# More rows fetched one by one, two gather buffers and undivided VectorE copies in a recommendation kernel

## The chip, the cores and the metric

The kernel runs on one core of one Trainium2 chip. The metric is the device time of one execution in microseconds (us), as the median of several runs.

## The reference

For each of 2048 samples, 26 embedding rows of 64 numbers are looked up in 26 tables of 12,500 rows. A 27th vector comes from the price by a dense layer. All products of two of the 27 vectors go, with the output of a small network over the dense vector, through two last layers.

```python
emb = emb_tables[jnp.arange(NUM_FIELDS)[:, None], x_cat]      # 26 x 2048 x 64
emb = jnp.transpose(emb, (1, 0, 2))
dense_embed = price[:, None] @ Wp + bp
feats = jnp.concatenate([emb, dense_embed[:, None, :]], axis=1)
gram = jnp.einsum('bid,bjd->bij', feats, feats)
interactions = gram[:, _IU, _JU]                              # 351 pairs
h = jax.nn.relu(dense_embed @ W1 + b1)
dense_out = jax.nn.relu(h @ W2 + b2)
concat = jnp.concatenate([interactions, dense_out], axis=1)
t = jax.nn.relu(concat @ Wt1 + bt1)
out = (t @ Wt2 + bt2)[:, 0]
```

## The kernel before, in words

The 2048 samples are 16 tiles of 128. Sample s of a tile sits on partition s, and for each tile and each of the 26 fields one column of 64 numbers per partition has to be fetched. Most columns are fetched by GpSimd with one indirect DMA each (`gather`, L274), which takes its 128 row numbers from `row_idx`. Fifteen of the 416 columns, all of them field 24 or field 25, are instead fetched row by row: SyncE issues 128 single DMAs of 256 bytes for field 25 of the nine tiles in `SP_TILES`, and ScalarE does so for field 24 of the six tiles in `ACT_TILES` (`fetch_rows`, L175 loads up to 32 addresses into registers, L178 issues the DMAs). The addresses lie on one partition in `by_row_at`, and VectorE computes them at the start from a second copy of the indices (`row_addresses`).

ScalarE can't issue its rows in one go, since it has other work: `fetch_some(n)` issues the next n rows of its list at fixed places of its program. There are 24 rows ahead of tile 0, and in each tile 32 after the first chunk, 12 after the second, 12 after the first round of copies and 8 after the second, until the list of 768 rows is empty.

A tile is worked on in this order. Its columns come in two chunks (fields 0 to 13, fields 14 to 25). For each chunk TensorE transposes pairs of fields into `ps_trans` (L553). VectorE copies the even fields and ScalarE the odd ones into `feats` (`evacuate_chunk`, L212); both have to be done before the next chunk is transposed. ScalarE also writes the dense vector into `feats` (`dense_slots`, L313). Then come two rounds of Gram products: 32 matmuls into the four banks of `ps_gram` (L600), and 16 copies of 32x112 numbers out of it into `gram` (`evacuate_gram`, L203), eight by VectorE (quads 0, 1) and eight by ScalarE (quads 2, 3). The next round waits for all 16. `gathered` has one buffer, so GpSimd may fetch a chunk of tile t only once TensorE has transposed that chunk of tile t-1.

Tiles form batches (0-3, 4-7, 8-11, 12-13, 14-15). At the first tile of the next batch, between its first and second chunk, TensorE does `top_layer` for the batch before (L627, L632; two halves of 7 matmuls with 2 passes each), ScalarE applies the relu to the first half (L368), VectorE to the second (L501), and the scores follow (L653, L378). Tile 14 is done in four finer rounds (L621, L200). Tile 15 is laid out in four units of 32 samples, each with its own gathers, transposes (L574), round and copies (L198), so that little is left after the last gather. Each engine has a fixed program order, and engines wait for each other only through semaphores.

Of the kernel before, what the change touches and what calls it, by code (L numbers as in the profile page):

```python
# [8 lines left out]
P = 128  # L9
# [34 lines left out]
ROW_TILES = SP_TILES + ACT_TILES  # L44
PAIRS = sorted(set(ROW_TILES))
REGS = 32
FIRST_ROWS, AFTER_FIRST_CHUNK, AFTER_CHUNKS, AFTER_ROUND = 24, 32, 12, (12, 8)
# [12 lines left out]
def rec_kernel(nc, price, x_cat, x_rows, table, consts, w1, w2, wt1_pairs, wt1_dense, out):  # L60
# [3 lines left out]
    with ExitStack() as ctx:  # L64
# [47 lines left out]
        by_row_loaded = sem("by_row_loaded")  # L112
        sp_rows_made = sem("sp_rows_made")
        act_rows_made = sem("act_rows_made")
        sp_fetched = [sem(f"sp_fetched{n}") for n in range(len(SP_TILES))]
        act_fetched = [sem(f"act_fetched{n}") for n in range(len(ACT_TILES))]
        base_made = sem("base_made")
        idx_step = sem("idx_step")
# [38 lines left out]
        def by_gpsimd(t, f):  # L157
            return not (f == SP_FIELD and t in SP_TILES or f == ACT_FIELD and t in ACT_TILES)

# [12 lines left out]
        def fetch_rows(eng, name, t, f, at, p0, n, done):  # L172

            row_of = [eng.alloc_register(f"{name}_{t}_{p0 + k}") for k in range(n)]
            eng.load(row_of, by_row_at[:, at + p0:at + p0 + n])  # L175
            for k in range(n):
                row = eng.snap(row_of[k], min_val=0, max_val=(FIELDS * VOCAB - 1) * ROW_BYTES, donate=True)
                eng.dma_start(field_at(t, f, 1)[p0 + k:p0 + k + 1, :].bitcast(u8), table_bytes[:, bass.ds(row, ROW_BYTES)])\  # L178
                    .then_inc(done, 16)
# [35 lines left out]
        def evacuate_unit(copy, n, kk):  # L215
# [29 lines left out]
        def _(sp):  # L245
            sp.dma_start(raw_idx[:, 0:FIELDS], x_cat[:, 0:FIELDS]).then_inc(first_idx_loaded, 16)
            sp.dma_start(raw_idx[:, FIELDS:], x_cat[:, FIELDS:]).then_inc(idx_loaded, 16)
            sp.dma_start(by_row_raw[:, :], x_rows).then_inc(by_row_loaded, 16)
# [3 lines left out]
            for n, t in enumerate(SP_TILES):  # L252
                sp.wait_ge(sp_rows_made, 1 if n == 0 else 2)
                for p0 in range(0, P, REGS):
                    fetch_rows(sp, "sp_row", t, SP_FIELD, n * P, p0, REGS, sp_fetched[n])
# [8 lines left out]
        def _(pool):  # L264
# [13 lines left out]
            for t in range(LAST):  # L278
# [4 lines left out]
                for c, (f0, f1) in enumerate(CHUNKS):  # L283
# [3 lines left out]
                    if t > 0:  # L287
                        pool.wait_ge(chunk_transposed[c], t)
# [4 lines left out]
            pool.wait_ge(rows_made, 2 + 3 * UNITS)  # L293
            pool.wait_ge(chunk_transposed[0], LAST)
            for n in range(UNITS):
                if n == 2:
                    pool.wait_ge(chunk_transposed[1], LAST)
                for col in UNIT_COLS[n]:
                    gather(LAST, col, unit_gathered[n])

        @block.scalar
        def _(act):
# [13 lines left out]
            issued = [0]  # L316
# [448 lines left out]
```

## Time and profile before

| | |
|---|---|
| median of 3 runs | 525.09 us (524.4 to 525.5) |
| profiled execution | 524.21 us, of which the span of the trace is 522.3 us |
| GpSimd busy | 381.2 us (73%) |
| TensorE busy | 247.1 us (47%) |
| ScalarE busy | 167.7 us (32%) |
| VectorE busy | 153.5 us (29%) |

Issuing a DMA is not counted as busy time. A gather counts with what GpSimd does for it (0.95 us), but a row DMA that SyncE or ScalarE issues shows only as a row of the queue (SPq, ACTq). So the busy time of ScalarE tells less than half of what fills it. The span is 1.9 us shorter than the time of the same execution.

### The profile page before, as it was taken

How to read it: one execution, taken by the hardware profiler on the slowest of the kernel's cores; microseconds unless marked ns; L12 is line 12 of the kernel's file. 1: busy time of each engine (PE TensorE's matmuls, PEld its weight loads, DVE VectorE, ACT ScalarE, POOL GpSimd, SP SyncE). 2: the span in 40 equal slices, each digit the busy share in tenths (PEclk: the TensorE clock that was granted, in tenths of full speed). 3: DMA queues.
4: the chain of work that ended last, by engine and by line, in shares of the span. 5: the costliest groups of instructions: out<-in, count | busy, mean ns of one | idle time of the engine just before them, and what ended most of it. 6: DMA issues, size and time to landing. Idle time of an engine off the chain costs nothing.

```text
span 522.3 us, 8323 instructions
## 1 busy us (share of the span) xinstructions
PE 247.1 (47%) x1481; PEld 181.6 (35%) x1481; DVE 153.5 (29%) x399; ACT 167.7 (32%) x413; POOL 381.2 (73%) x408
## 2 busy tenths in 40 slices
PE   0004436154548661432516954151432894469487
PEld 0003324132333350422415434050422543356375
DVE  6203303123140141241304024042241315332753
ACT  0032513335142141242404225042242425342743
POOL 6777777777777777777777776777777777777770
PEclk9999755666578855566656976555566896668789
DMA  6333332333323333333333332333333333332110
GB/s 191 26 28 29 28 29 28 28 29 28 28 28 29 29 28 28 30 27 30 28 30 26 29 28 24 29 30 27 28 28 30 27 29 27 29 28 27 28 26 4
DMA packets 17754, 16.52 MB, mean 32 GB/s; under 512 B 10772, under 2 KB 11028, under 8 KB 17574
## 3 DMA queue, kind: packets, MB, share of 16 engines
q0 software_dynamic: 12832, 13.17, 30.6%
q1 hardware_dynamic: 2886, 2.49, 1.6%
q10 hardware_dynamic: 1984, 0.34, 0.4%
q14 instruction: 40, 0.33, 0.3%
q8 instruction: 12, 0.20, 0.2%
HBM read 15.95 MB, written 0.01 MB: 31 GB/s over the span
## 4 chain that ended last, share of the span: by engine, by line
ACTq 31%; POOL 19%; PE 19%; issue 16%; ACT 13%; DMA 2%; DVE 1%; POOLq 0%
ACTq L178 26%; POOL gathered L274 18%; PE ps_gram L600 10%; ACT gram L203 9%; PE ps_mlp L632 5%; ACTq L175 4%; ACT feats L212 2%; ACT feats L313 1%; DMA gathered<-in_table,row_idx 1%; PE ps_trans L553 1%; PE ps_trans L632 1%; PE ps_mlp L627 0%; ACT dense_out L363 0%; PE ps_mlp L584 0%; DMA raw_idx<-in_x_cat 0%
## 5 line engine op out<-in xcount | busy, mean ns | idle before, releaser
L274 POOL DMA_INDIRECT gathered<-in_table,row_idx x394 | 373.8, 949 | 124.9 <-issue 118.9
L600 PE MATMUL ps_gram<-feats 64*128 64x128 f32 x896 | 101.9, 414 | 137.3 <-issue 79.3
L600 PEld LDWEIGHTS ps_gram<-feats 64*128 64x128 f32 x896 | 95.4, 317 | 150.9 <-issue 144.3
L203 DVE COPY gram<-ps_gram 32x112 f32<-32x112 f32 x224 | 80.4, 359 | 197.5 <-PE ps_gram L600 194.8
L203 ACT COPY gram<-ps_gram 32x112 f32<-32x112 f32 x224 | 80.9, 361 | 116.3 <-PE ps_gram L600 84.2
L553 PE MATMUL ps_trans<-ident,gathered 128*128 128x128 f32 x184 | 39.9, 378 | 119.2 <-DMA gathered<-in_table,row_idx 71.9
L212 ACT COPY feats<-ps_trans 64x448 f32<-64x448 f32 (+1 forms) x60 | 34.1, 569 | 164.5 <-issue 121.6
L553 PEld LDWEIGHTS ps_trans<-ident,gathered 128*128 128x128 f32 x184 | 30.6, 197 | 131.3 <-issue 131.2
L212 DVE COPY feats<-ps_trans 64x448 f32<-64x448 f32 (+1 forms) x60 | 36.3, 604 | 94.8 <-PE ps_trans L553 94.0
L632 PE MATMUL ps_mlp<-gram,wt1p_sb 128*128 128x512 f32 (+2 forms) x140 | 54.7, 552 | 1.7 <-ACT gram L203 1.7
L632 PEld LDWEIGHTS ps_mlp<-gram,wt1p_sb 128*128 128x128 f32 x140 | 28.8, 222 | 27.6 <-issue 22.5
L501 DVE TENSOR_SCALAR top<-ps_mlp,consts_sb 128x512 f32<-128x512 f32 (+1 forms) x4 | 2.7, 684 | 52.0 <-PE ps_mlp L632 52.0
L313 ACT ACTIVATE feats<-price_bc,consts_sb 64x64 f32<-64x64 f32 x30 | 14.7, 491 | 0.8
L621 PE MATMUL ps_gram<-feats 64*128 64x128 f32 x128 | 9.9, 301 | 10.1 <-ACT feats L222 4.4
L621 PEld LDWEIGHTS ps_gram<-feats 64*128 64x128 f32 x128 | 8.6, 204 | 11.9 <-DVE feats L222 7.8
L627 PE MATMUL ps_mlp<-dense_out,wt1d_sb 64*128 64x512 f32 (+2 forms) x20 | 10.0, 586 | 3.5 <-ACT dense_out L363 3.5
L198 DVE COPY gram<-ps_gram 32x56 f32<-32x56 f32 x32 | 8.2, 256 | 10.2 <-PE ps_gram L621 9.8
L198 ACT COPY gram<-ps_gram 32x56 f32<-32x56 f32 x32 | 8.3, 259 | 6.3 <-PE ps_gram L621 6.0
L212 ACT ACT_TABLE_LOAD x1 | 1.3, 1283 | 26.9 <-issue 26.9
L200 DVE COPY gram<-ps_gram 32x56 f32<-32x56 f32 x32 | 8.3, 258 | 1.7 <-PE ps_gram L621 1.3
L200 ACT COPY gram<-ps_gram 32x56 f32<-32x56 f32 x32 | 8.3, 260 | 1.3 <-PE ps_gram L621 0.9
L368 ACT ACTIVATE top<-ps_mlp,consts_sb 128x512 f32<-128x512 f32 (+1 forms) x4 | 2.5, 634 | 18.0 <-PE ps_mlp L632 18.0
(54 smaller groups left out, 100.3 us busy)
## 6 DMA issues: line engine op xcount, KB each, us to landing
pairs_of<-in_table SPq DMA_DIRECT2D x1152, 0.2 KB
pairs_of<-in_table ACTq DMA_DIRECT2D x768, 0.2 KB
gathered<-in_table,row_idx POOLq DMA_INDIRECT x394, 3.4
price_bc<-in_price SPq DMA_DIRECT2D x1, 1024.0 KB, 5.7
wt1p_sb<-in_wt_pairs SPq DMA_DIRECT2D x1, 896.0 KB, 7.8
raw_idx<-in_x_cat SPq DMA_DIRECT2D x1, 195.0 KB, 2.7
pairs_of<-in_table,row_idx POOLq DMA_INDIRECT x7
w_sb<-in_w ACTq DMA_DIRECT2D x2, 32.0 KB, 3.1
```

The costliest lines, as they stand in the source:

```text
L175: eng.load(row_of, by_row_at[:, at + p0:at + p0 + n])
L178: eng.dma_start(field_at(t, f, 1)[p0 + k:p0 + k + 1, :].bitcast(u8), table_bytes[:, bass.ds(row, ROW_BYTES)])\
L198: last = copy(gram_unit[to, w, k, r, :, :, :, s], fine_from[part, r % 2, :, :, s, 0:SLABS, c])
L200: last = copy(gram_to[to, w, k, :, FINE_RG * r:FINE_RG * (r + 1), :, s], fine_from[part, r % 2, :, :, s, 0:SLABS, c])
L203: last = copy(gram_to[to, w, k, :, RG * r:RG * (r + 1), :, s], gram_from[part, :, :, s, 0:SLABS, c])
L212: last = copy(feats[D * h:D * (h + 1), :, 1 + f0 + q:f1 + q:2], src[D * q:D * (q + 1), h, :, :])
L274: pool.indirect_dma_start(out=field_at(t, f, 1), out_offset=None, in_=rows, in_offset=bass.IndirectOffsetOnAxis(ap=row_idx[:, at:at + 1], ...
L313: return nc.scalar.activation(dst, price_bc[part, first:first + n], ACT.Identity, bias=const(BP, part), scale=const(WP, part))
L553: last = nc.tensor.transpose(ps_trans[:, to + k * P:to + (k + 1) * P], field_at(t, f, 2), ident[:, :])
L600: last = nc.tensor.matmul(ps_gram[:, out_at:out_at + P], group, group, start=True, stop=True)
L621: last = nc.tensor.matmul(ps_gram[:, to:to + P], group, group, start=True, stop=True)
L632: last = nc.tensor.matmul(to, wt1p_sb[:, j * TM1 + m * P:j * TM1 + (m + 1) * P], gram[:, at + part.start:at + part.stop], start=False, sto ...
```

## The change

1. Seventeen columns instead of fifteen are fetched row by row. SyncE has 1208 rows: field 25 of eight tiles, 104 rows of tile 14 and 80 rows of tile 15. ScalarE has 968 rows: field 24 of tiles 2, 4, 6, 7, 9, 11, 13, and the remaining 24 and 48 rows of field 25 of tiles 14 and 15. GpSimd issues 399 gathers, before 401.
2. ScalarE issues 36 rows ahead of tile 0 (now before it waits for the small inputs), then 32 after the first chunk and 40 after the second chunk of each tile; none between the rounds of copies.
3. In tiles 0 to 11 VectorE makes all 16 copies of each Gram round. From tile 12 on the two engines share them as before.
4. `gathered` has two buffers: a chunk of tile t waits for the transposes of tile t-2.
5. The addresses on one partition come from 17 matmuls, which turn columns of `row_idx` into rows, and five scalings by VectorE; the second copy of the indices is gone. The clamp of the indices takes three instructions instead of four, and for the long part it works in PSUM. The base numbers of tile 15 are laid out once.
6. The order of fields in the units of tile 15 changes, and with it the address pattern of the copies in `evacuate_unit`.

```diff
-BUFFERS = 1
+BUFFERS = 2
-SP_TILES = (2, 4, 5, 7, 8, 10, 11, 13, 14)
-ACT_TILES = (2, 4, 6, 8, 10, 12)
+SPLIT_ROWS = {LAST - 1: 104, LAST: 80}
+SP_TILES = (2, 4, 5, 7, 8, 10, 11, 13)
+ACT_TILES = (2, 4, 6, 7, 9, 11, 13)
+SP_ROWS = [(t, SP_FIELD, 0, P) for t in SP_TILES] + [(t, SP_FIELD, 0, n) for t, n in SPLIT_ROWS.items()]
+ACT_ROWS = [(t, ACT_FIELD, 0, P) for t in ACT_TILES] + [(t, SP_FIELD, n, P - n) for t, n in SPLIT_ROWS.items()]
-FIRST_ROWS, AFTER_FIRST_CHUNK, AFTER_CHUNKS, AFTER_ROUND = 24, 32, 12, (12, 8)
+VECTOR_ALONE = 12
+FIRST_ROWS, AFTER_FIRST_CHUNK, AFTER_CHUNKS = 36, 32, 40
...
-                    if t > 0:
-                        pool.wait_ge(chunk_transposed[c], t)
+                    if t >= BUFFERS:
+                        pool.wait_ge(chunk_transposed[c], t - BUFFERS + 1)
...
             def fetch_some(n):
-                if issued[0] == 0:
-                    act.wait_ge(act_rows_made, 1)
-                while n > 0 and issued[0] < len(ACT_TILES) * P:
-                    k, p0 = divmod(issued[0], P)
-                    now = min(n, P - p0, REGS)
-                    fetch_rows(act, "act_row", ACT_TILES[k], ACT_FIELD, (len(SP_TILES) + k) * P, p0, now, act_fetched[k])
-                    issued[0] += now
-                    n -= now
+                for t, f, first, rows in ACT_ROWS:
+                    while n > 0 and issued[t, f, first, rows] < rows:
+                        done = issued[t, f, first, rows]
+                        now = min(n, rows - done, REGS)
+                        act.wait_ge(addresses_made, address_group(t, f) + 1)
+                        fetch_rows(act, "act_row", t, f, first + done, now)
+                        issued[t, f, first, rows] += now
+                        n -= now
...
                 fetch_some(AFTER_CHUNKS)
-                for r in range(ROUNDS if t < LAST - 1 else FINE_ROUNDS):
-                    gram_round(r, t)
-                    if r < ROUNDS:
-                        fetch_some(AFTER_ROUND[r])
+                if t >= VECTOR_ALONE:
+                    for r in range(ROUNDS if t < LAST - 1 else FINE_ROUNDS):
+                        gram_round(r, t)
...
             def gram_round(r, t):
                 dve.wait_ge(gram_done, rounds_before(t) + r + 1)
-                evacuate_gram(nc.vector.tensor_copy, t, r, (0, 1)).then_inc(gram_evac_dve, 1)
+                evacuate_gram(nc.vector.tensor_copy, t, r, range(GROUP) if t < VECTOR_ALONE else (0, 1))\
+                    .then_inc(gram_evac_dve, 1)
...
+            pe.wait_ge(by_row_picked, 1)
+            for k, (t, f) in enumerate(BY_ROW):
+                col = 2 * t + f - ACT_FIELD
+                summed = nc.tensor.matmul(address_sums(k * P, (k + 1) * P), by_row_idx[:, col:col + 1], ident[:, :],
+                                          start=True, stop=True)
+                if (k + 1) % AT_ONCE == 0 or k == len(BY_ROW) - 1:
+                    summed.then_inc(addresses_summed, 1)
+            pe.wait_ge(addresses_made, ADDRESS_GROUPS)
...
             def wait_gram_evac(n):
                 if n > 0:
                     pe.wait_ge(gram_evac_dve, n)
-                    pe.wait_ge(gram_evac_act, n)
+                if n > ROUNDS * VECTOR_ALONE:
+                    pe.wait_ge(gram_evac_act, n - ROUNDS * VECTOR_ALONE)
```

On ScalarE (ACT), before, tile 11 ends with its last eight rows and 16 copies, and tile 12, which begins with the copies of the first chunk and has the top layer, holds no row at all:

```order
L175 TENSOR_LOAD by_row_at
L178 DMA pairs_of<-in_table 1x256 x8
L203 COPY gram<-ps_gram 32x2x8x7 x16
L212 COPY feats<-ps_trans 64x64x7 x2
L313 ACTIVATE feats<-price_bc,consts_sb 64x64 x2
L368 ACTIVATE top<-ps_mlp,consts_sb 128x512
L212 COPY feats<-ps_trans 64x64x6 x2
L378 ACTIVATE scores<-ps_mlp,consts_sb 1x512
L203 COPY gram<-ps_gram 32x2x8x7 x16
```

The same place on ScalarE after the change: tile 12 from the copies of its first chunk to the copies of its Gram rounds.

```order
L223 COPY feats<-ps_trans 64x64x7 x2
L320 ACTIVATE feats<-price_bc,consts_sb 64x64 x2
L375 ACTIVATE top<-ps_mlp,consts_sb 128x512
L186 TENSOR_LOAD by_row_at
L189 DMA pairs_of<-in_table 1x256 x20
L186 TENSOR_LOAD by_row_at
L189 DMA pairs_of<-in_table 1x256 x12
L223 COPY feats<-ps_trans 64x64x6 x2
L385 ACTIVATE scores<-ps_mlp,consts_sb 1x512
L186 TENSOR_LOAD by_row_at
L189 DMA pairs_of<-in_table 1x256 x32
L186 TENSOR_LOAD by_row_at
```

What moved: 68 rows and four loads now stand in tile 12, 32 rows between the relu and the copies of the second chunk, and 36 (the last four behind a load of their own, just past the end of the piece) between those and the 16 Gram copies.

On ScalarE in a middle tile, before (tile 10, from the copies of its first chunk to the end of its rows; the 12 rows after the second chunk stand as one load here):

```order
L212 COPY feats<-ps_trans 64x64x7 x2
L313 ACTIVATE feats<-price_bc,consts_sb 64x64 x2
L175 TENSOR_LOAD by_row_at
L178 DMA pairs_of<-in_table 1x256 x32
L212 COPY feats<-ps_trans 64x64x6 x2
L175 TENSOR_LOAD by_row_at
L178 DMA pairs_of<-in_table 1x256 x12
L203 COPY gram<-ps_gram 32x2x8x7 x8
L175 TENSOR_LOAD by_row_at
L178 DMA pairs_of<-in_table 1x256 x12
L203 COPY gram<-ps_gram 32x2x8x7 x8
```

And after the change, tile 11 of ScalarE, the middle tile with the most loads:

```order
L223 COPY feats<-ps_trans 64x64x7 x2
L320 ACTIVATE feats<-price_bc,consts_sb 64x64 x2
L186 TENSOR_LOAD by_row_at
L189 DMA pairs_of<-in_table 1x256 x32
L223 COPY feats<-ps_trans 64x64x6 x2
L186 TENSOR_LOAD by_row_at
L189 DMA pairs_of<-in_table 1x256 x32
L186 TENSOR_LOAD by_row_at
L189 DMA pairs_of<-in_table 1x256 x4
```

What moved: the Gram copies are gone from ScalarE, and all rows of the tile's second half stand in one run (32+8 in most tiles, 32+4+4 in this one) ahead of the next tile's first copies.

## Rows read from the trace of the kernel before

**Rows 1.** The page: granted TensorE clock in 40 slices of 13 us, tenths of full.

```profile
PEclk9999755666578855566656976555566896668789
```

**Rows 2.** Timeline of GpSimd: start, duration, what, idle time before it.

```profile
3.92 1.10 POOL L274 DMA_INDIRECT gathered<-in_table,row_idx  x1 [2.32 <-DVE row_idx L448]
...
12.61 1.56 POOL L274 DMA_INDIRECT gathered<-in_table,row_idx  x1 [0.30 <-issue]
...
493.15 0.94 POOL L274 DMA_INDIRECT gathered<-in_table,row_idx  x1 [0.30 <-issue]
```

**Rows 3.** Who waited for whom: total us, times, longest.

```profile
POOL gathered L274 <- issue: 118.9, 389, 0.5
POOL gathered L274 <- PE ps_trans L553: 3.6, 4, 1.9
```

**Rows 4.** The chain that ended last, its last gather: start, duration, what.

```profile
506.87 0.94 POOL gathered L274
```

**Rows 5.** Timeline of ScalarE: one run of 12 rows in tile 9, then tile 10.

```profile
338.03 4.97 ACTq L178 DMA_DIRECT2D pairs_of<-in_table  x12
...
354.62 1.26 ACT L212 COPY feats<-ps_trans 64x448 f32<-64x448 f32 x2 [1.65 <-issue]
355.90 1.01 ACT L313 ACTIVATE feats<-price_bc,consts_sb 64x64 f32<-64x64 f32 x2
356.95 10.56 ACTq L178 DMA_DIRECT2D pairs_of<-in_table  x32
367.55 1.03 ACT L212 COPY feats<-ps_trans 64x384 f32<-64x384 f32 x2 [10.64 <-issue]
368.69 4.25 ACTq L178 DMA_DIRECT2D pairs_of<-in_table  x12
...
384.57 1.26 ACT L212 COPY feats<-ps_trans 64x448 f32<-64x448 f32 x2 [1.65 <-issue]
```

**Rows 6.** Loads and row DMAs by source line: ns min/median/max, first and last start.

```profile
L175 ACTq TENSOR_LOAD <-by_row_at x52: 580/954/2295, 17.1 to 397.5; - x52
L178 SPq DMA_DIRECT2D pairs_of<-in_table x1152: 227/228/457, 7.6 to 465.7; - x192
```

**Rows 7.** Timeline of TensorE: a Gram round of tile 9.

```profile
346.02 3.79 PE L600 MATMUL ps_gram<-feats 64*128 64x128 f32 x32 [4.01 <-ACT gram L203]
```

**Rows 8.** Timeline of VectorE: eight copies of one Gram round.

```profile
311.85 2.83 DVE L203 COPY gram<-ps_gram 32x112 f32<-32x112 f32 x8 [9.04 <-PE ps_gram L600]
```

**Rows 9.** Timeline of ScalarE, the top layer in tile 8, and the start of tiles 5 and 12.

```profile
197.38 1.26 ACT L212 COPY feats<-ps_trans 64x448 f32<-64x448 f32 x2 [1.94 <-issue]
...
293.71 0.69 ACT L368 ACTIVATE top<-ps_mlp,consts_sb 128x512 f32<-128x512 f32 x1 [2.41 <-PE ps_mlp L632]
...
306.89 1.03 ACT L212 COPY feats<-ps_trans 64x384 f32<-64x384 f32 x2 [12.50 <-issue]
...
412.29 1.28 ACT L212 COPY feats<-ps_trans 64x448 f32<-64x448 f32 x2
```

**Rows 10.** Timeline of TensorE: tile 8's top layer, then from tile 13 to the last unit.

```profile
287.42 6.25 PE L632 MATMUL ps_mlp<-gram,wt1p_sb 128*128 128x512 f32 x14 [0.46 <-ACT gram L203]
...
437.48 1.75 PE L553 MATMUL ps_trans<-ident,gathered 128*128 128x128 f32 x7
447.08 1.30 PE L553 MATMUL ps_trans<-ident,gathered 128*128 128x128 f32 x5 [7.85 <-DMA pairs_of<-in_table,row_idx]
...
456.83 3.55 PE L600 MATMUL ps_gram<-feats 64*128 64x128 f32 x32 [3.34 <-ACT gram L203]
465.37 1.73 PE L553 MATMUL ps_trans<-ident,gathered 128*128 128x128 f32 x7 [4.99 <-DMA gathered<-in_table,row_idx]
...
487.41 0.55 PE L574 MATMUL ps_trans<-ident,gathered 128*128 128x128 f32 x3
...
495.52 0.87 PE L574 MATMUL ps_trans<-ident,gathered 128*128 128x128 f32 x3 [0.94 <-DMA gathered<-in_table,row_idx]
...
510.66 0.55 PE L574 MATMUL ps_trans<-ident,gathered 128*128 128x128 f32 x3 [0.28 <-DMA gathered<-in_table,row_idx]
```

More of the change, by code:

```diff
@@ L111, in rec_kernel @@
         idx_loaded = sem("idx_loaded")
[L112 to L116, printed above, removed]
+        by_row_picked = sem("by_row_picked")
+        addresses_summed = sem("addresses_summed")
+        addresses_made = sem("addresses_made")
+        row_fetched = {at: sem(f"row_fetched_{at[0]}_{at[1]}") for at in BY_ROW}
         base_made = sem("base_made")
+        last_base_made = sem("last_base_made")
         idx_step = sem("idx_step")
@@ L157, in by_gpsimd @@
         def by_gpsimd(t, f):
-            return not (f == SP_FIELD and t in SP_TILES or f == ACT_FIELD and t in ACT_TILES)
+            return (t, f) not in BY_ROW
         def gathers_before(c, t):
@@ L247, in _ @@
             sp.dma_start(raw_idx[:, FIELDS:], x_cat[:, FIELDS:]).then_inc(idx_loaded, 16)
-            sp.dma_start(by_row_raw[:, :], x_rows).then_inc(by_row_loaded, 16)
             sp.dma_start(price_bc[:, :], price.rearrange("(o b) -> o b", o=1).to_broadcast([P, BATCH])).then_inc(price_loaded, 16)
             sp.dma_start(wt1p_sb[:, :], wt1_pairs).then_inc(pairs_loaded, 16)
[L252 to L255, printed above, removed]
+            for t, f, first, n in SP_ROWS:
+                sp.wait_ge(addresses_made, address_group(t, f) + 1)
+                for p0 in range(first, first + n, REGS):
+                    fetch_rows(sp, "sp_row", t, f, p0, min(REGS, first + n - p0))
             for late in range(2):
@@ L559, in transpose_chunk @@
                 pe.wait_ge(chunk_gathered[c], 16 * gathers_before(c, t + 1))
-                if t in SP_TILES and f1 > SP_FIELD:
-                    pe.wait_ge(sp_fetched[SP_TILES.index(t)], 16 * P)
-                if t in ACT_TILES and f1 > ACT_FIELD:
-                    pe.wait_ge(act_fetched[ACT_TILES.index(t)], 16 * P)
+                for f in range(f0, f1):
+                    if not by_gpsimd(t, f):
+                        pe.wait_ge(row_fetched[t, f], 16 * P)
                 transpose_fields(t, f0, f1, 0).then_inc(chunk_transposed[c], 1)
@@ L569, in transpose_unit @@
                 keep_warm(n, n % 2)
-                pe.wait_ge(unit_gathered[n], 16 * len(UNIT_COLS[n]))
+                pe.wait_ge(unit_gathered[n], 16 * sum(by_gpsimd(LAST, col) for col in UNIT_COLS[n]))
+                for col in UNIT_COLS[n]:
+                    if not by_gpsimd(LAST, col):
+                        pe.wait_ge(row_fetched[LAST, col], 16 * P)
                 base = (LAST % BUFFERS) * ROW
                 for m in range(COLS // 2):
-                    at, to = base + UNIT_COLS[n][2 * m] * D, BANK * (n % 2) + m * P
-                    last = nc.tensor.transpose(ps_trans[:, to:to + P], gathered[:, at:at + 2 * D], ident[:, :])
+                    to = BANK * (n % 2) + m * P
+                    last = nc.tensor.transpose(ps_trans[:, to:to + P], field_at(LAST, UNIT_COLS[n][2 * m], 2), ident[:, :])
                 if n % 2 == 0:
@@ L737 @@
     last = cat[:, -1].reshape(FIELDS, UNITS, 2, SIDE)
-    own = last[:SHARED].reshape(COLS, UNITS, UNITS, 2, SIDE).transpose(1, 3, 4, 2, 0).reshape(P, UNITS, COLS)
+    own = last[:SHARED].reshape(UNITS, COLS, UNITS, 2, SIDE).transpose(0, 3, 4, 2, 1).reshape(P, UNITS, COLS)
     shared = last[SHARED:].reshape(2, 2, 2, 2, SIDE).transpose(2, 0, 3, 4, 1).reshape(P, 2)
```

125 lines of the change are left out of this document (65 added, 60 removed).

## The prediction

> **What bounds the kernel now.** I read the timeline of GpSimd first, since most columns come through it. Its gathers start every 1.247 us ((506.87-493.15)/11, [rows 2, 4]) from 3.92 to 506.87 us, and 400 such steps are 498.8 of these 503 us. The rest is about 2 us in the first 15 us, where single gathers take up to 1.56 us [rows 2], and waits: 389 of its idle times are the plain 0.3 us of issue, and four, 3.6 us together, wait for the transposes that free the only buffer [rows 3]. So GpSimd sets the end, and behind its last gather 15.4 us are left.
>
> The second view is the timeline of ScalarE, and it says that something else is almost as long. I call the start of a tile's first ScalarE copies A0 and that of its second A1. In tile 10, A0 is at 354.62, 32 rows are issued, A1 is at 367.55, and the next A0 at 384.57 [rows 5]: 29.95 us a tile, filled with 64 row issues and 16 copies, where GpSimd needs 30 to 31 us for 24 or 25 gathers. That a single buffer costs GpSimd only four waits shows how close the race is. Whatever lengthens the path of ScalarE and TensorE is therefore what I have to price.
>
> **Terms.** One row costs ScalarE 10.56/32 = 0.33 us; a 32-row run with its load takes 12.93 us from A0 to A1, the copies hidden in the load [rows 5]. A run of 8 costs a load (0.7, between the least and the median) and 8 x 0.33: 3.3 us; a run of 4 costs 2.0. A field border inside a run adds 0.7 (4.97 against 4.25 us for 12 rows) [rows 5, 6]. A Gram round is 3.8 us of matmuls in the middle [rows 7], a first-chunk transpose 1.75 [rows 10]. Sixteen copies by VectorE alone do not occur in the trace. Bounds: 5.7 us (twice the 2.83 of eight, [rows 8]) if they run as now, and 2.83 if one engine could do 16 in the time of 8, for which no row speaks; I take 5.8, since eight also take a little longer in other rounds.
>
> **Gathers.** Two fewer, 2.5 us; the four waits go, 2.4 us beyond issue; the first gather can start 0.2 us sooner (one dependent VectorE step less). Of the 2 us at the start I keep 0.7, bounds 0 and 2.0: the gathers stretch where VectorE works on long vectors. The last gather then starts at 3.7+0.7+398 x 1.247 = 500.7 instead of 506.87. *SBUF — State Buffer* in the Trainium skill (SBUF: two separate sides) says that VectorE and GpSimd share a port pair as an exclusive lock, taken by operations with two inputs in SBUF or in a two-port mode. The stretched gathers beside such operations agree, and by that rule the copies from PSUM, now doubled, cost the gathers nothing; mid-kernel gathers take 0.94 us [rows 2].
>
> **The middle tiles.** After A1 there are two legs up to the next A0. ScalarE: 32 rows 12.9 and 8 rows 3.3, together 16.2. TensorE and VectorE: copies 1.03, round 3.8, copies 5.8, round 3.8, transposes 1.75, some 0.3 of handing over, together 16.5. So a tile is 12.9+16.5 = 29.4 us, half a microsecond less than before: eight more rows have replaced the copies. The first four tiles are paced by gathers and the same ScalarE load, and tile 4's top layer, waiting 0.5 us longer for VectorE, starts about where it did; I put A0 of tile 5 where it was, 197.4 [rows 9].
>
> Three steps bring A0 of tile 8 to 285.6. Its top layer needs the copies of tile 7's second round, which VectorE ends 20.55 after A1 of tile 7 (copies 1.03, then round, 16 copies, round, 16 copies, and handing over), so at 269.1+20.55 = 289.7; before, eight copies sufficed. Its first half takes 6.3 us [rows 10], relu at 295.9, then 13.2 to A1 as before (293.71 to 306.89, [rows 9]) and 0.7 for a border: 309.8. A0 of tile 9 is 326.3, of 10 355.7, of 11 385.8 (border), and of 12 415.6 (A1 398.7, then runs of 32, 4 and 4: 16.9). Before it was 412.3 [rows 9]. A lag of up to 20 us behind the gathers does not stop GpSimd, for with two buffers it may be a whole tile ahead.
>
> **Tile 12** is where I expect the change to be decided. Before, the list of rows was empty by then, the last load being at 397.5 [rows 6], and from A0 at 412.29 to the transposes of tile 13 took 25 us [rows 9, 10]. Now 36+12x72 = 900 of 968 rows are out, and 68 are left, ahead of Gram copies that ScalarE shares again from this tile on. VectorE ends tile 11 at 398.7+20.55 = 419.3; relu 425.6; 32 rows with a border, A1 at 439.5. Then 36 rows, 12.9+2.0, to 454.4; only now ScalarE's copies of the first round, 3.0, and TensorE's second round, 3.9. Tile 13's transposes start at 461.3, against 437.48.
>
> **From there to the end** nothing waits for gathers any more. ScalarE's copies of the round end at 464.4, the chunk's at 465.7, the second transposes start at 465.8. From there to tile 14's first is 13.3 us (447.08 to 456.83+3.55): 479.1. Tile 14 to the first unit took 22.04, of which 0.3 waited, and gets 0.5 more since ScalarE's copies are not done ahead: 501.4. First to last unit took 23.25 with 1.2 of waiting for gathers: 523.4. The last unit to the end is 11.64 [rows 10]. That is a span of 535.1 and a time of 537.0; the profiled execution lay 0.9 under the median, so **537.9 us**.
>
> **What is free.** SyncE: 1152 rows took 458.1 us, so 12.7 us per 32 with a load [rows 6]; 1208 rows in 39 runs take 484, and starting near 12 us (indices landed by 5, some 5 us of VectorE and TensorE steps, a load) they end near 496, with the last unit not wanted before 523. If TensorE were on time (504) there would be 8 us left. Later addresses (matmuls, the memset of `feats` ahead of the scalings) cost ScalarE's first 36 rows nothing, as they end by about 25 us, when the first chunk is there. The new copy pattern of the units has the same element counts.
>
> *Trainium Kernel Development and Optimization* in the Trainium skill (Key Constraints) says that issuing DMAs from several engines only saves the sequencer's issue time. That speaks against this change: a column moved off GpSimd frees 1.25 us there and fills some 42 us (128 x 0.33) of another queue, and ScalarE's is the one that the copies stand behind.
>
> **Rivals.** (a) *The gathers stay the bound.* Last gather 500.7, last unit 3.8 later at 504.5, span 516.1, median 518.9: faster. It needs the last unit 18.9 us sooner than my path. For it speaks that GpSimd bounds the kernel today. A row cost of 0.26 us would do: near the 0.23 that the queue shows for one row DMA alone [rows 6], cycles of 27 us, the lag of each top layer gone before the next. Against it, the long runs of the trace cost 0.33 apiece and more [rows 5].
> (b) *TensorE at its upper clock.* Slices 6 to 39 mostly show 0.5 to 0.7 of full [rows 1], a mix of the two levels 1.2 and 2.4 GHz, and the 3.8 us rounds are at the lower. At 2.1 us each round, both top layers start 3.4 us sooner, and tiles 4, 12 and 13 give as much again: about 17 us less, 521. Against it, TensorE will idle longer between rounds than now.
> (c) *Slower still.* ScalarE's rows in one unbroken run could cost 0.35 instead of 0.33, or 16 copies 6.2: 1 to 1.4 us per tile more, 545 to 550.
> (d) *The delays cancel.* If the path is about 12.7 us shorter than I sum it, the last unit is ready at 510.7 and nothing changes: 525.
>
> **Numbers.** My case 0.73, with its own range 530 to 546; (a) 0.12, (b) 0.05, (c) 0.06, (d) 0.04. A measurement tells about 0.2% (1 us) from no change. Faster: (a) and (b), 0.17. Same: most of (d), 0.03. Slower: the rest, 0.80. The range reaches from 524 to 547, leaving out (a), (b) and half of (c).
>
> **What would show it.** In the changed trace, GpSimd's last gather near 500.7, without waits. A0 of tiles 5, 8, 12 near 197, 286, 416, 29.4 us apart between. In tile 12 two row runs around A1, ScalarE's Gram copies ending near 457, and the first transposes of tile 13 near 461, some 28 us after their gathers. A last unit that waits for no DMA, near 523, and a chain that ended last without GpSimd in its final 20 us. I am wrong if a run of 32 rows takes 10 us with its load, if Gram rounds in the middle take 2.1 us, or if GpSimd's last gather ends less than 5 us ahead of the last unit's transposes.

## The result and the profile after

The changed kernel takes 541.71 us (median of 4 runs, 540.58 to 544.45). The kernel before, run beside it, took 524.88. The ratio is 1.0328, with a 95% interval of 1.0287 to 1.0368. The profiled execution took 541.54 us, with a span of 539.4.

The page after the change: the granted clock in 40 slices, then the engines' shares of the chain that ended last, then the group of VectorE's Gram copies.

```profile
PEclk9656757556679665656567956565655895659679
PE 31%; DVE 23%; issue 15%; POOL 6%; ACTq 4%; ACT 4%; DMA 1%; POOLq 0%
L214 DVE COPY gram<-ps_gram 32x112 f32<-32x112 f32 x416 | 144.9, 348 | 190.0 <-PE ps_gram L620 181.2
```

GpSimd, which set the end before [rows 4], holds 6% of this chain, and TensorE and VectorE hold more than half. The clock is still the mix of its two levels, as in [rows 1].

Who waited for whom after the change (total us, times, longest):

```profile
ACT feats L223 <- issue: 215.2, 17, 16.3
POOL gathered L284 <- issue: 125.5, 377, 5.8
PE ps_gram L620 <- DVE gram L214: 71.2, 12, 5.9
```

The waits of GpSimd for transposes [rows 3] have shrunk to one of 0.3 us. But its "issue" row has a longest entry of 5.8 us, where it was 0.5. The timeline of GpSimd shows where that is:

```profile
3.67 1.10 POOL L284 DMA_INDIRECT gathered<-in_table,row_idx  x1 [2.07 <-DVE row_idx L465]
...
271.05 0.94 POOL L284 DMA_INDIRECT gathered<-in_table,row_idx  x1 [0.30 <-issue]
277.84 0.94 POOL L284 DMA_INDIRECT gathered<-in_table,row_idx  x1 [5.85 <-issue]
...
416.54 0.94 POOL L284 DMA_INDIRECT gathered<-in_table,row_idx  x1 [0.30 <-issue]
422.65 0.94 POOL L284 DMA_INDIRECT gathered<-in_table,row_idx  x1 [5.17 <-issue]
...
511.28 0.94 POOL L284 DMA_INDIRECT pairs_of<-in_table,row_idx  x1 [0.30 <-issue]
```

Two steps take 6.79 and 6.11 us instead of 1.25, ahead of gathers 215 and 327 (counted from 0), and the profile names nothing that GpSimd waits for. I call them the pauses. They cost 10.4 us of gathering, and they stood in no sum.

ScalarE's timeline: the first copies (x448) of tiles 5, 8, 9, 10 and 12 are what the prediction calls A0, the second ones (x384) A1.

```profile
195.99 1.26 ACT L223 COPY feats<-ps_trans 64x448 f32<-64x448 f32 x2 [15.30 <-PE ps_trans L571]
...
286.37 1.26 ACT L223 COPY feats<-ps_trans 64x448 f32<-64x448 f32 x2 [15.89 <-issue]
...
328.82 1.26 ACT L223 COPY feats<-ps_trans 64x448 f32<-64x448 f32 x2 [15.14 <-PE ps_trans L571]
...
331.15 10.59 ACTq L189 DMA_DIRECT2D pairs_of<-in_table  x32
341.78 1.03 ACT L223 COPY feats<-ps_trans 64x384 f32<-64x384 f32 x2 [10.68 <-issue]
...
344.12 14.86 ACTq L189 DMA_DIRECT2D pairs_of<-in_table  x40
359.02 1.26 ACT L223 COPY feats<-ps_trans 64x448 f32<-64x448 f32 x2 [16.20 <-issue]
...
420.17 1.26 ACT L223 COPY feats<-ps_trans 64x448 f32<-64x448 f32 x2 [16.28 <-issue]
...
431.20 0.69 ACT L375 ACTIVATE top<-ps_mlp,consts_sb 128x512 f32<-128x512 f32 x1 [8.73 <-PE ps_mlp L652]
...
432.72 12.26 ACTq L189 DMA_DIRECT2D pairs_of<-in_table  x32
445.03 1.03 ACT L223 COPY feats<-ps_trans 64x384 f32<-64x384 f32 x2 [13.14 <-issue]
...
447.35 12.74 ACTq L189 DMA_DIRECT2D pairs_of<-in_table  x36
460.12 2.84 ACT L214 COPY gram<-ps_gram 32x112 f32<-32x112 f32 x8 [13.36 <-issue]
```

In the middle (tile 9, 328.82 to 359.02) a tile takes 30.20 us, before 29.95 [rows 5]. In tile 12 ScalarE's copies of the first Gram round start only at 460.12, behind 68 rows. TensorE's timeline shows who waits for them:

```profile
289.66 8.49 PE L652 MATMUL ps_mlp<-gram,wt1p_sb 128*128 128x512 f32 x14 [3.83 <-DVE gram L214]
...
446.16 3.79 PE L620 MATMUL ps_gram<-feats 64*128 64x128 f32 x32 [5.28 <-issue]
463.11 3.79 PE L620 MATMUL ps_gram<-feats 64*128 64x128 f32 x32 [13.16 <-ACT gram L214]
466.83 1.64 PE L571 MATMUL ps_trans<-ident,gathered 128*128 128x128 f32 x7
...
484.73 1.23 PE L571 MATMUL ps_trans<-ident,gathered 128*128 128x128 f32 x7
...
504.99 0.90 PE L594 MATMUL ps_trans<-ident,gathered 128*128 128x128 f32 x3
...
527.76 0.38 PE L594 MATMUL ps_trans<-ident,gathered 128*128 128x128 f32 x2
```

The second round waits 13.16 us for ScalarE's copies. Tile 13's transposes start at 466.83 (before 437.48), those of the last unit at 527.76 (before 510.66, [rows 10]), and neither waits for a DMA. From tile 8's A0 to tile 9's, 42.45 us pass, and from tile 12's A0 to tile 13's transposes 46.66 us, before 25.2 [rows 9, 10]. Tile 12 alone thus costs 21.5 us more; of the whole lateness of tile 13, 29.4 us, 12.3 are taken up behind it, where the kernel before waited 13.8 us for DMAs (7.85, 4.99 and 0.94 in [rows 10]) and this one doesn't, and 17.1 reach the end. The last wait of TensorE for a DMA in the changed kernel ends at 133.94 us, long before the pauses, so the pauses hold up nothing on this path.

VectorE, all 16 copies of a round, twice the eight of [rows 8] and little more:

```profile
193.61 5.77 DVE L214 COPY gram<-ps_gram 32x112 f32<-32x112 f32 x16 [3.97 <-PE ps_gram L620]
```

### The profile page after: what moved, and what is told of

Its sections match the earlier page's. It is cut to its first block, busy times and chain, and to the rows that moved or that the text cites. A ratio compares the mean times of both kernels' runs of the same rounds, so it can differ in the third digit from the quotient of the medians.

```text
span 539.4 us, 8883 instructions
## 1 busy us (share of the span) xinstructions
PE 252.5 (47%) x1515; PEld 185.0 (34%) x1515; DVE 213.8 (40%) x581; ACT 98.9 (18%) x221; POOL 377.4 (70%) x406
## 4 chain that ended last, share of the span: by engine, by line
PE 31%; DVE 23%; issue 15%; POOL 6%; ACTq 4%; ACT 4%; DMA 1%; POOLq 0%
DVE gram L214 19%; PE ps_gram L620 14%; PE ps_mlp L652 9%; POOL gathered L284 6%; ACTq L189 4%; DVE feats L223 3%; PE ps_trans L571 3%; PE ps_gram L641 2%; ACT gram L214 2%; ACT gram L211 1%; DMA gathered<-in_table,row_idx 1%; PE ps_trans L554 1%; PE ps_mlp L673 1%; PE ps_trans L652 1%; PE ps_mlp L647 1%
## 5 line engine op out<-in xcount | busy, mean ns | idle before, releaser
L284 POOL DMA_INDIRECT gathered<-in_table,row_idx x392 | 370.0, 944 | 131.9 <-issue 125.5
L214 DVE COPY gram<-ps_gram 32x112 f32<-32x112 f32 x416 | 144.9, 348 | 190.0 <-PE ps_gram L620 181.2
L620 PE MATMUL ps_gram<-feats 64*128 64x128 f32 x896 | 104.3, 421 | 159.3 <-DVE gram L214 71.2
L620 PEld LDWEIGHTS ps_gram<-feats 64*128 64x128 f32 x896 | 97.5, 323 | 173.5 <-issue 169.2
L571 PE MATMUL ps_trans<-ident,gathered 128*128 128x128 f32 x184 | 36.5, 353 | 97.7 <-DMA gathered<-in_table,row_idx 49.1
L571 PEld LDWEIGHTS ps_trans<-ident,gathered 128*128 128x128 f32 x184 | 27.6, 181 | 108.9 <-issue 68.3
L652 PEld LDWEIGHTS ps_mlp<-gram,wt1p_sb 128*128 128x128 f32 x140 | 27.7, 214 | 37.8 <-issue 22.5
L214 ACT COPY gram<-ps_gram 32x112 f32<-32x112 f32 x32 | 11.6, 362 | 25.9 <-issue 13.4
L641 PE MATMUL ps_gram<-feats 64*128 64x128 f32 x128 | 11.5, 335 | 9.1 <-ACT feats L233 3.3
L370 ACT ACTIVATE dense_out<-ps_mlp,consts_sb 64x512 f32<-64x512 f32 x4 | 2.7, 682 | 63.5 <-issue 48.0
L641 PEld LDWEIGHTS ps_gram<-feats 64*128 64x128 f32 x128 | 10.1, 236 | 11.2 <-DVE feats L233 7.0
L542 PE MATMUL ps_gram<-ident,by_row_idx 128*1 128x128 f32 x32 | 5.8, 370 | 6.3 <-DVE by_row_idx L481 6.3
```

Source lines behind the costliest of these rows:

```text
L214: last = copy(gram_to[to, w, k, :, RG * r:RG * (r + 1), :, s], gram_from[part, :, :, s, 0:SLABS, c])
L284: pool.indirect_dma_start(out=field_at(t, f, 1), out_offset=None, in_=rows, in_offset=bass.IndirectOffsetOnAxis(ap=row_idx[:, at:at + 1], ...
L571: last = nc.tensor.transpose(ps_trans[:, to + k * P:to + (k + 1) * P], field_at(t, f, 2), ident[:, :])
L620: last = nc.tensor.matmul(ps_gram[:, out_at:out_at + P], group, group, start=True, stop=True)
L641: last = nc.tensor.matmul(ps_gram[:, to:to + P], group, group, start=True, stop=True)
L652: last = nc.tensor.matmul(to, wt1p_sb[:, j * TM1 + m * P:j * TM1 + (m + 1) * P], gram[:, at + part.start:at + part.stop], start=False, sto ...
```

## The experiments

Each edit is against the changed kernel unless it says otherwise. The kernel before took 524.16 us beside the first four kernels, 524.25 beside the next three and 524.04 beside the two after them; the last three kernels ran once each.

### VectorE alone in tile 12 too

```diff
-VECTOR_ALONE = 12
+VECTOR_ALONE = 13
```

> The changed kernel with one constant changed: VectorE makes all 16 Gram copies in tile 12 too, so that no copy of ScalarE stands behind the 68 rows there. Theory M (the loss is made in tile 12, where ScalarE's share of the copies waits for 36 rows): the second Gram round of tile 12 starts at about 456 instead of 463.1, the second transposes of tile 13 4 to 5 us sooner than 471.3; about 537 us (535 to 539) instead of 541.7. Rival V (VectorE making the copies alone is what costs, 2.9 us more in each round): one more tile of it makes it no faster, 541 to 548. Rival G (GpSimd's two unexplained pauses of 5.5 and 4.9 us set the end): no change, 541 to 542.

536.09 us (534.69 to 536.42), ratio 1.0223 (1.0186 to 1.0260). TensorE's timeline, tile 13:

```profile
461.71 1.52 PE L571 MATMUL ps_trans<-ident,gathered 128*128 128x128 f32 x7
468.94 1.32 PE L571 MATMUL ps_trans<-ident,gathered 128*128 128x128 f32 x5 [5.71 <-DVE feats L223]
```

The first transposes come 5.1 us sooner, since no round waits for ScalarE. More VectorE work in one tile makes the kernel faster, so the sixteen copies are not what costs. The gathers don't set the end either: their pauses stayed (last gather 511.99) and the time still fell. But the rows remain ahead of the next tile's copies, and most of the loss remains.

### Without the split columns

```diff
-SPLIT_ROWS = {LAST - 1: 104, LAST: 80}
+SPLIT_ROWS = {}
```

Fifteen columns, with 896 rows on ScalarE instead of 968 and none of them in tile 12.

> The changed kernel with fifteen columns by row instead of seventeen: field 25 of tiles 14 and 15 goes back to GpSimd, 401 gathers. ScalarE's list has 896 rows and is empty before tile 12. Everything else, VectorE alone in tiles 0 to 11, the 32 and 40 rows, two buffers, stays. Theory M: tile 12 has no row, the transposes of tile 13 start at 451 instead of 466.8, the last unit at 512, near the gathers' own bound of 507; about 526 us (523 to 529), so most of the loss is gone with 72 of ScalarE's rows. Rival V (VectorE alone): tiles 0 to 11 are as they were and most of the loss stays, 536 or more. Rival G: as now or slower, 541 to 545, since GpSimd has two more gathers.

532.68 us (531.00 to 533.66), ratio 1.0165 (1.0124 to 1.0206). TensorE's timeline, tiles 13 and 14 and the last unit, and then GpSimd's last gather:

```profile
449.18 1.75 PE L571 MATMUL ps_trans<-ident,gathered 128*128 128x128 f32 x7
...
470.86 1.52 PE L571 MATMUL ps_trans<-ident,gathered 128*128 128x128 f32 x6 [4.19 <-DMA gathered<-in_table,row_idx]
...
518.66 0.55 PE L594 MATMUL ps_trans<-ident,gathered 128*128 128x128 f32 x3
```

```profile
514.87 0.94 POOL L284 DMA_INDIRECT gathered<-in_table,row_idx  x1 [0.30 <-issue]
```

Tile 13 starts 17.7 us sooner, near the 451 expected. ScalarE's list is 72 rows shorter by then, 68 in tile 12 and the last four in tile 11. A0 of tile 12 is at 418.14, 2.0 us sooner, and the other 15.6 us are what the 68 rows of tile 12 cost. The time was 6.7 us above the 526 expected. I had left out the pauses (steps of 7.14 and 6.95 us here), and once the path is shorter they count: tile 14 now waits for gathers.

### Shared copies and the rows in more places

```diff
-VECTOR_ALONE = 12
-FIRST_ROWS, AFTER_FIRST_CHUNK, AFTER_CHUNKS = 36, 32, 40
+VECTOR_ALONE = 0
+FIRST_ROWS, AFTER_FIRST_CHUNK, AFTER_CHUNKS, AFTER_ROUND = 36, 32, 12, (12, 8)
...
+                        if r < ROUNDS:
+                            fetch_some(AFTER_ROUND[r])
```

> The changed kernel with the copies of every Gram round shared as before, and ScalarE's rows at the places of before (32, 12, 12 and 8 a tile, 36 ahead), still 968 of them. 36+12x64 = 804 rows are out by tile 12, so 164 are left for tiles 12 to 14. Theory M (rows left for the last tiles cost): tile 5 starts near 197, tile 12 near 412 as before, but tile 13 near 450 and the last unit near 530: 536 to 548. Rival V (VectorE alone is what costs): back to about the time of before, 522 to 528.

547.53 us (546.64 to 551.13), ratio 1.0471 (1.0419 to 1.0523), 5.8 us slower than the changed kernel. The edit changes who copies and where the rows stand, and the timelines of ScalarE and of TensorE in tile 13 show a cost of the places:

```profile
455.10 11.45 ACTq L189 DMA_DIRECT2D pairs_of<-in_table  x32
```

```profile
466.64 1.30 PE L573 MATMUL ps_trans<-ident,gathered 128*128 128x128 f32 x5 [17.20 <-DMA gathered<-in_table,row_idx]
```

Tile 12 starts at 417.88, 2.3 us sooner than in the changed kernel, with 96 rows fewer issued by then. By the end of tile 12 868 rows are out (36+13x64), but tile 13's own column ends with row 896. Its last 28 rows are in the run above, and TensorE waits 17.20 us, until that run has ended. The profile names gathers there, but those of tile 13 had all started before 444, so the wait was for these rows. Rows left for the end thus cost also because a tile needs them itself. Whether sharing the copies costs anything with 968 rows isn't shown.

### The kernel before with two gather buffers

```diff
-BUFFERS = 1
+BUFFERS = 2
```

> The kernel before with two gather buffers and nothing else of the change. Both theories: the four waits of GpSimd go (2.4 us beyond issue), the last gather starts at about 504.5 instead of 506.9, and the time is about 522.5 us (521 to 524.5). If instead running further ahead disturbs GpSimd (pauses as in the changed kernel), 525 or more.

521.15 us (520.03 to 521.67), ratio 0.9937 (0.9919 to 0.9954); last gather at 505.15, and no pause. This part of the change gains 3.0 us by itself, as much as the last gather moves (from 508.12, see the part on the prediction).

### The rows and copies of before, with the new start

Rows, shared copies and places as before; two buffers, addresses by matmul and the new layout of tile 15 as changed.

```diff
-SPLIT_ROWS = {LAST - 1: 104, LAST: 80}
-SP_TILES = (2, 4, 5, 7, 8, 10, 11, 13)
-ACT_TILES = (2, 4, 6, 7, 9, 11, 13)
+SPLIT_ROWS = {}
+SP_TILES = (2, 4, 5, 7, 8, 10, 11, 13, 14)
+ACT_TILES = (2, 4, 6, 8, 10, 12)
...
-VECTOR_ALONE = 12
-FIRST_ROWS, AFTER_FIRST_CHUNK, AFTER_CHUNKS = 36, 32, 40
+VECTOR_ALONE = 0
+FIRST_ROWS, AFTER_FIRST_CHUNK, AFTER_CHUNKS, AFTER_ROUND = 24, 32, 12, (12, 8)
...
+                        if r < ROUNDS:
+                            fetch_some(AFTER_ROUND[r])
```

> Two buffers and the new start (addresses by matmul, shorter clamp) of the change, with the rows of before (fifteen columns, nine and six tiles, 24 rows ahead, 32, 12, 12 and 8 a tile) and every Gram copy shared. Against the kernel before with two buffers alone (521.15) only the start and the layout of tile 15 differ: the changed kernel lost 0.15 us in its first gathers instead of 2.0 and began 0.2 sooner, so 519 us (518 to 520). Rival P (the pauses of GpSimd that all four kernels with the new start show, at gathers 215 and 327, and the two with the old start don't, belong to the new start, not to the rows): two pauses of 1 to 7 us are in the trace here too, and the time is 521 to 527.

519.44 us (519.14 to 519.93), ratio 0.9904 (0.9871 to 0.9936); last gather at 503.29, again no pause. The new start gains another 1.7 us (1.9 in the last gather), and the pauses don't come from it.

### One column more, half of it on each queue

Against the one just shown: field 25 of tile 15, 64 rows by each engine.

```diff
-SPLIT_ROWS = {}
+SPLIT_ROWS = {LAST: 64}
...
-FIRST_ROWS, AFTER_FIRST_CHUNK, AFTER_CHUNKS, AFTER_ROUND = 24, 32, 12, (12, 8)
+FIRST_ROWS, AFTER_FIRST_CHUNK, AFTER_CHUNKS, AFTER_ROUND = 36, 32, 12, (12, 8)
```

> As c1_old_rows_new_start, with a sixteenth column by row: field 25 of tile 15, 64 rows by SyncE and 64 by ScalarE, and 36 rows ahead instead of 24. 400 gathers. ScalarE has 28 rows left in tile 12, where they cost about 3 us that tile 13's wait for its gathers absorbs. Theory M: 1.2 us less than c1 (517.5 to 519.5 without pauses), since GpSimd sets the end as long as few rows are left for tile 12. If more rows cost by themselves: slower than c1.

519.37 us (518.72 to 519.50), ratio 0.9901 (0.9869 to 0.9933). The last gather starts at 502.08, 1.2 us sooner. The last unit comes only 0.7 us sooner (505.03) and no longer waits for a DMA, and the median is the same. So even a single column more brought nothing that can be measured. The rule on issuing from several engines that the prediction weighed (*Trainium Kernel Development and Optimization* in the Trainium skill, Key Constraints) fits this run: 1.2 us of issue were saved on GpSimd, and nothing more.

### The rows of a top-layer tile ahead of the relu

Against the kernel with VectorE alone in tile 12 too:

```diff
+                fetch_some(AFTER_FIRST_CHUNK)
                 if first:
                     top_relu(n - 1)
-                fetch_some(AFTER_FIRST_CHUNK)
```

> The changed kernel with VectorE alone in tile 12 too (as a1, 536.1), and ScalarE's 32 rows after a first chunk ahead of the relu of the top layer instead of behind it. ScalarE waits 6.7, 9.5 and 8.7 us for the sums there in tiles 4, 8 and 12 of the changed kernel. Theory L (the path through ScalarE is the bound, and the three top layers make its lag): 5 to 6 us per top layer come back, the last unit is then bound by GpSimd with its pauses: 528 to 530 us, 519 to 521 if the pauses are gone. Rival V (VectorE's copies, 19% of the chain): moving ScalarE's rows brings nothing, 535 to 537.

529.34 us (528.03 to 530.77), ratio 1.0095 (1.0063 to 1.0126). TensorE's timeline, tiles 13 and 14 and the last unit:

```profile
446.54 1.75 PE L571 MATMUL ps_trans<-ident,gathered 128*128 128x128 f32 x7
...
469.81 1.73 PE L571 MATMUL ps_trans<-ident,gathered 128*128 128x128 f32 x7 [2.27 <-DMA gathered<-in_table,row_idx]
...
515.03 0.38 PE L594 MATMUL ps_trans<-ident,gathered 128*128 128x128 f32 x2
```

The same rows, issued while ScalarE would wait for the top layer, cost 6.8 us less, and tile 13 starts 15.2 us sooner. They move in tiles 4, 8 and 12 alike: A0 of tile 12 is already 8.6 us sooner (413.81, with the rows behind the relu 422.37), and 6.6 us are won in tile 12. Tile 14 again waits for gathers, of which the last starts at 511.34 with the pauses still there.

### The old columns, with VectorE alone

```diff
-SPLIT_ROWS = {LAST - 1: 104, LAST: 80}
-SP_TILES = (2, 4, 5, 7, 8, 10, 11, 13)
-ACT_TILES = (2, 4, 6, 7, 9, 11, 13)
+SPLIT_ROWS = {}
+SP_TILES = (2, 4, 5, 7, 8, 10, 11, 13, 14)
+ACT_TILES = (2, 4, 6, 8, 10, 12)
```

> The changed kernel with the fifteen columns of before (nine tiles for SyncE, six for ScalarE, 768 rows, so that ScalarE's list is empty in tile 10). VectorE alone in tiles 0 to 11, 32 and 40 rows a tile, two buffers and the new start stay. Against c1_old_rows_new_start (519.4) only VectorE alone and the places of the rows differ. Theory M/L (only rows left for the end of ScalarE's list cost, and its lag is caught up as soon as it has none): GpSimd is the bound, 519 to 521 us if it makes no pauses, 529 to 533 with two pauses of 5 us. Rival V (VectorE alone costs by itself): slower than c1 by more than its pauses explain. Rival P2 (the pauses come with VectorE alone or with 40 rows in one go): pauses at gathers 215 and 327. Rival P3 (they come with the set of tiles that are fetched by row): none.

519.18 us (519.15 to 519.87), ratio 0.9910 (0.9878 to 0.9942). TensorE's timeline, tiles 13 and 14 and the last unit:

```profile
438.82 0.98 PE L571 MATMUL ps_trans<-ident,gathered 128*128 128x128 f32 x7
...
460.86 1.73 PE L571 MATMUL ps_trans<-ident,gathered 128*128 128x128 f32 x7 [3.60 <-DMA gathered<-in_table,row_idx]
...
505.83 0.55 PE L594 MATMUL ps_trans<-ident,gathered 128*128 128x128 f32 x3
```

This is the run that isolates the cause. Everything of the change is in it but the columns and their 200 additional rows on ScalarE (and 56 on SyncE). It equals the kernel with shared copies (519.44), so VectorE alone and the runs of 32 and 40 rows cost nothing while the list is short. Against the changed kernel, 22.5 us lie in the choice of columns. Nor do the pauses come with VectorE alone or with long runs, since there are none here.

### Seventeen columns from other tiles

Against the kernel with the rows ahead of the relu: 960 rows on ScalarE, 60 of them in tile 12.

```diff
-SPLIT_ROWS = {LAST - 1: 104, LAST: 80}
-SP_TILES = (2, 4, 5, 7, 8, 10, 11, 13)
-ACT_TILES = (2, 4, 6, 7, 9, 11, 13)
+SPLIT_ROWS = {LAST: 64}
+SP_TILES = (2, 4, 5, 7, 8, 10, 11, 13, 14)
+ACT_TILES = (2, 4, 6, 8, 10, 12, 13)
```

> As d1_rows_before_relu (529.3), with another set of seventeen columns: SyncE field 25 of nine tiles and 64 rows of tile 15, ScalarE field 24 of tiles 2, 4, 6, 8, 10, 12, 13 and the other 64 rows of tile 15; 960 rows, 60 of them in tile 12. 399 gathers. If the pauses come with the set of tiles (P3): none here, last gather near 501, 518 to 519.5 us, under c1 and c2. If they come with VectorE alone or the 40 rows (P2): last gather near 511 and 528 to 530 us.

523.29 us (521.11 to 524.72), ratio 0.9981 (0.9961 to 1.0001): missed by some 4 us. TensorE's timeline, tile 14 and the last unit:

```profile
469.24 1.75 PE L571 MATMUL ps_trans<-ident,gathered 128*128 128x128 f32 x7
...
510.93 0.38 PE L594 MATMUL ps_trans<-ident,gathered 128*128 128x128 f32 x2
```

There are no pauses, and the last gather starts at 501.09, as I expected. But the last unit is at 510.93, 9.8 us behind it, and waits for no DMA. Seventeen columns in the best order that I found still leave the path of ScalarE and TensorE later than the gathers. Two gathers fewer don't pay for 192 rows more.

### Where the pauses come from

Three kernels, one run each. The first two are against the old columns with VectorE alone, the third against the first. The first takes ScalarE's tiles from the changed kernel, the second SyncE's:

```diff
-ACT_TILES = (2, 4, 6, 8, 10, 12)
+ACT_TILES = (2, 4, 6, 7, 9, 11)
```

> The kernel of f1_old_rows, in which ScalarE's six fetched columns are taken from tiles 2, 4, 6, 7, 9 and 11 (the changed kernel's set without its last tile) instead of those of before; rows, copies, buffers and start stay. If the two pauses of GpSimd (5 to 7 us each, with no wait in the trace) come with ScalarE's set of tiles, gathers show gaps of 4 to 8 us in two places, the last gather starts near 514 and the time is about 529. If they come with SyncE's set or with the number of columns, there are none, the last gather starts near 503.5 and the time is 518.5 to 520.

```diff
-SP_TILES = (2, 4, 5, 7, 8, 10, 11, 13, 14)
+SP_TILES = (2, 4, 5, 7, 8, 10, 11, 13)
```

> The kernel of f1_old_rows, in which SyncE fetches eight columns (tiles 2, 4, 5, 7, 8, 10, 11, 13) instead of nine, tile 14 left to the gathers; the rest stays. One gather more at 1.25 us gives a last gather near 504.5 and a time of 519.5 to 521 if SyncE's set does not matter for the pauses; if it brings them, gaps of 4 to 8 us in two places, a last gather near 515 and about 530.

```diff
+        spare = sb("spare", [P, 32])
...
+            for i in range(20):
+                pool.memset(spare[:, i:i + 1], 0.0)
```

> The kernel of p1_other_scalar_tiles, in which GpSimd clears twenty single columns of an unused tile before its first gather (about 0.6 us, inside its 2.1 us of waiting for the indices); nothing else is changed, but each gather stands twenty instructions further on in GpSimd's program. If the pauses hang on the place in GpSimd's program at which it is when code has to be fetched, they sit at other gathers than numbers 215 and 327 (some gathers earlier) or are gone (then about 519.5 us). If they hang on the number of gathers issued, or on what the other engines do at that moment, the gap of some 8 us stays at gather 215, the smaller one at 327, and the time stays near 527.6.

The three took 527.61, 521.73 and 527.45 us, the kernel before 526.03 beside the first two and 525.34 beside the third. GpSimd's timeline in the first:

```profile
271.03 0.94 POOL L284 DMA_INDIRECT gathered<-in_table,row_idx  x1 [0.30 <-issue]
279.31 0.94 POOL L284 DMA_INDIRECT gathered<-in_table,row_idx  x1 [7.34 <-issue]
...
511.62 0.94 POOL L284 DMA_INDIRECT gathered<-in_table,row_idx  x1 [0.31 <-issue]
```

And in the third:

```profile
271.08 0.94 POOL L287 DMA_INDIRECT gathered<-in_table,row_idx  x1 [0.30 <-issue]
279.27 0.94 POOL L287 DMA_INDIRECT gathered<-in_table,row_idx  x1 [7.25 <-issue]
```

With ScalarE's set of tiles alone changed, with as many gathers, rows and copies as before, the long pause is back at gather 215 and a shorter one (a step of 2.55 us) at gather 327, and the last gather comes 8.3 us later (511.62 against 503.31). With SyncE's set changed there is none. Twenty instructions more ahead of the gathers on GpSimd moved neither pause (the second step is 2.54 us), so a shift of twenty instructions in GpSimd's program doesn't matter. One thing remains mixed: GpSimd leaves out the columns that ScalarE fetches, so ScalarE's set of tiles changes GpSimd's own list too. The second chunk of tile 8 begins with gather 214 in the kernels with pauses and with 215 in those without. Which of the two lists matters was not separated.

## Why the prediction was right

It said 537.9 us, and the kernel takes 541.7, slower by the mechanism that it named. Step by step:

**Tiles 0 to 8.** A0 of tile 5 was put at 197.4 and is at 195.99; that of tile 8 at 285.6 and is at 286.37. The top layer of tile 8 starts at 289.66, where VectorE's 16 copies put it (289.7); that it fits to the tenth is luck, since A1 of tile 7 was 0.3 us late (269.44) and the leg behind it 0.3 shorter. Sixteen copies take 5.77 us, the 5.8 taken. The lower bound of 2.83 is ruled out.

**Two terms too small.** The first half of the top layer was taken at 6.3 us from [rows 10] and took 8.49 in tile 8 and 7.97 in tile 12. The windows of the changed kernel over these two halves (length, busy time of PE, PEld, DVE, ACT and POOL, granted clock, DMA share, GB/s):

```profile
289.66:298.15 8.49, 8.49 (x15) 3.48 (x15) 1.23 (x2) 0.00 (x0) 6.36 (x8) 0.74 0.36 26
423.19:431.16 7.97, 7.97 (x15) 3.24 (x15) 1.22 (x2) 0.00 (x0) 6.06 (x7) 0.79 0.32 28
```

The granted clock is 0.74 and 0.79: part of each half ran at 1.2 GHz, the rest at 2.4. Before, the half in tile 8 (287.42 to 293.67) was granted 1.00 throughout. There TensorE had been busy 4.96 of the 5.4 us ahead of it; now it idles 3.83 us ahead, waiting for VectorE's copies. I moved the start and kept the duration of a stretch at the upper clock; that is 2.2 and 1.7 us. ScalarE's leg behind A1 was summed as 16.2 and took 17.24: the row of 40 lasts 14.86, of which 32 rows are 10.59, so that 8 rows with their load cost 4.27 and not 3.3. A middle tile takes 30.2 and not 29.4. Together they bring A0 of tile 12 to 420.17 instead of 415.6.

**Tile 12** decided it, as said: two runs of rows around A1, ScalarE's Gram copies behind them, and 46.66 us to tile 13's transposes, where I had 45.7. From there each step kept 3.6 to 5.6 us of lateness: 466.83 (461.3 predicted), 484.73 (479.1), 504.99 (501.4), 527.76 (523.4), and 11.6 us behind the last, as taken. The runs show that this place was the right one: without the 68 rows tile 12 is 15.6 us shorter, and with its 32 rows ahead of the relu 6.6. One term behind it was too long: tile 14 up to the first unit was taken at 22.3 us and took 20.26. The first half of its top layer took 3.26 us at a granted clock of 1.00; before it took 5.98 at 0.54.

**Gathers.** The last one was predicted at 500.7 and starts at 511.28. The 0.7 us that I kept for the start was 0.15 (one step of 1.40, the others 1.25), a plain step was 1.249 us and not 1.247 (0.8 in all), and the pauses of 10.4 us were in no sum. The kernel before was misread, too: [rows 4] is not its last gather but the last but one, since its chain puts the last one down as its DMA.

```profile
506.87 0.94 POOL gathered L274
...
508.12 2.49 DMA gathered<-in_table,row_idx
```

So the last gather before started at 508.12, 14.2 us ahead of the end, and the last unit 2.5 us behind it, not 3.8. The 537.9 doesn't use this, but rival (a) does: by its own sum it should have said 517.7 and not 518.9. None of this touched the result, since the last unit came 16.5 us after the last gather's start, and 2.5 would do. Had the path been short, as in rival (a), the pauses would have counted: the kernel with the old number of rows and ScalarE's other tiles, whose last unit does wait for a gather, took 527.61 us in its one run. So the forecast of the gathers was wrong, and that it cost nothing is luck.

**Free of cost**, as said: SyncE's last row is issued at 493.2 (496 predicted), and the later addresses cost nothing.

The rivals fell by the same rows: (a) by a last unit that waits for no DMA; (b) by rounds that still take 3.79 us; (d) by 17 us that reach the end; (c) by 16 copies at 5.77, though its other price, dearer rows in long runs, was half right.

For the 16.8 us between the two kernels the runs give this account: two buffers -3.0 and the new start -1.7; VectorE alone with the longer runs about 0; the columns +22.5. The sum is +17.8, 1 us off, with medians from different series of runs. In the 22.5 us the path's share and the pauses can't be told apart by subtraction, since they lie beside each other; the path's is the one that ends last, and no wait of TensorE for a DMA lies behind the pauses.

**What stays open** is the cause of the pauses. Shown is that they come with ScalarE's set of tiles, stay at the same two gathers and don't move when twenty instructions are put ahead of them. Whether ScalarE's list or the change that it makes in GpSimd's own list stops GpSimd at gather 215, and how, isn't shown.

## What to carry to other kernels

Before moving work from the engine that bounds onto another engine's queue, sum that other engine's whole cycle, and look for the place where the work displaced lands at the end: here 200 rows of 0.33 us more ended as 68 rows ahead of copies for which TensorE waited. Issue such filler while the engine would wait anyway (ahead of the relu, not behind it: 6.8 us). Take a bundle of changes apart: two buffers and the new start gave 0.990 of the time before, and the seventeen columns gave back over four times what these gain.

## What the hardware showed that I had not expected

GpSimd stood still for 1.3 to 7 us beyond its step, at the same two gathers from one program to the next and with no wait in the trace, in all seven programs in which ScalarE fetches for tiles 2, 4, 6, 7, 9 and 11, and in none of the seven others.

In the first 15 us the gathers of the changed kernel lost 0.15 us, where those of before lost about 2 us [rows 2]. In the change, VectorE's long operation on the indices works in PSUM and the second copy of the indices is gone; which of the two did it was not tried. The Trainium skill's page *SBUF — State Buffer* (SBUF: two separate sides) says that the lock on the ports that VectorE and GpSimd share is taken by operations with two inputs in SBUF or in a two-port mode. By that rule the long operations on the indices, of which each now has one side in PSUM and at most one input in SBUF, cost the gathers nothing. This trace agrees: they run from 4.13 to 5.87 us, and the gathers beside and behind them keep their step of 1.25 us after the first.
